# Blocks of tokens turned by 32x32 squares and DMA instead of by TensorE, and two tiles of a macaron transformer block taken in another order

## The chip, the cores and the metric

The kernel runs on one core of one Trainium2 chip. Times are device microseconds (us) of whole executions; the profile and its trace are of one execution, taken by the hardware profiler. TensorE (PE) multiplies matrices, VectorE (DVE) does element-wise work and sums, ScalarE (ACT) activations, GpSimd (POOL) a few small steps, and SyncE (SP) issues most weight transfers. ACT issues transfers too: ACTq in the rows is ACT's sequencer issuing one. A lower time is better.

## The reference

```python
x = x + 0.5 * ffn(layernorm(x), W1, W2, W3)
x = x + attn(layernorm(x), wq, wk, wv, wo, inv_freq)
x = x + 0.5 * ffn(layernorm(x), W1, W2, W3)

def attn(x, ...):                      # x is 4 x 1024 x 512, 16 heads of 32
    q, k, v = x @ wq.T, x @ wk.T, x @ wv.T      # q and k rotated by position
    scores = einsum('bshd,bstd->bsht', q, k) / sqrt(32)   # heads against heads
    return (softmax(scores) @ v) @ wo.T         # of the same token

def ffn(x, W1, W2, W3):                # 512 -> 2048 -> 512
    hidden = silu(x @ W1.T) * (x @ W3.T)
    return fwht(hidden) @ W2.T         # Walsh-Hadamard, folded into W2 beforehand
```

Attention mixes the 16 heads of one token, never two tokens. All is fp32.

## The kernel before

**Work.** The 4096 tokens are 8 tiles of 512; a tile is 4 blocks of 128 tokens. `PASSES` (lines 35 and 36) lists 16 passes; (1, t) is the first feed-forward of tile t and (2, t) its second. I call the p-th entry pass p, from 0. A pass has 16 steps n; in a step PE does `up`, 24 matmuls into PSUM `gu` (gate half, then linear half), and then `down`, 12 matmuls into PSUM `acc`, of the step before. Each fp32 product is three matmuls: every operand is held as a high and a low part, and high-high, high-low and low-high are added.

**A step on the other engines.** When `up` of step n is finished, ACT has made `gated` (silu), DVE multiplies it (line 1584), ACT copies the high part of the hidden tile (line 1084), and DVE makes the low part (line 1591). PE needs the product of step n before `up` of step n + 2, and the low part for the last third of `down` of step n; at the end of a pass, for the whole of the last `down`.

**Attention on DVE.** The attention proper is done by DVE between these, in 512 units (a product and a reduction each, lines 1311 to 1325), three, two or one in a step: `units_by_step` spreads them by a table of costs, in which the other DVE work of a step is weighed too (`beside`, lines 106 to 110). An `exp` on ACT stands between a block's scores and its values.

**Gaps.** Between the passes PE does the projections of the next blocks: `query_key`, `value`, and for one tile `output`. `early_gap` and `late_gap` are the two forms; a pass is `LATE` when it is the second feed-forward of the tile whose attention output is projected in the gap just ahead of it, so that this tile must be normalized and turned inside the gap. Before, LATE is (5, 14, 15).

**Turning.** The projections need features on the partitions, the normalization has tokens there, so each tile and block is transposed once. There are two ways:
- a tile that is not LATE is turned by squares: DVE transposes 32x32 squares (line 1562, steps 8 and 9), ACT issues 16 DMAs from SBUF to SBUF that place them (line 945, four in each of steps 10 to 13), ACT makes the high part (line 952, step 14) and DVE the low one (line 1568, step 15). Attention outputs go the same way, but by a tensor in DRAM, `out_squares`: DVE transposes in place, ACT writes (line 957), and four DMAs read runs of 32 numbers (128 B) back (line 966).
- a block of 128 tokens, and everything of a LATE pass, is turned by PE with `transpose_sub` (line 689) and `transpose_bank` (line 669), 4 matmuls with the identity for a block and 16 for a tile; ACT takes the high part from PSUM (line 935), DVE the low one (line 1189). `early_subs(p)` are the first blocks of a gap whose input is there a pass ahead: DVE normalizes them in step 13 (`Q_APPLY`), and PE turns them between the last `up` and the last two `down`.

**The first gap.** POOL makes the low parts of the attention weights (line 1164); the last four of these, for `wo`, stand beside the first `rope` on DVE (lines 1281 to 1294), which rotates q and k.

## Time and profile before

| | |
|---|---|
| median of 3 runs | 2503.42 us (2503.2 to 2503.71) |
| the profiled execution, its own time | 2501.66 us |
| its span in the trace | 2499.8 us |
| PE busy | 2489.7 us (100%), 11111 matmuls |
| DVE busy | 2044.3 us (82%) |
| ACT busy | 530.2 us (21%) |
| DMA, q1 (SP) and q10 (ACT), share of 16 engines | 46.0% and 5.7% |
| TensorE clock granted | full throughout |

In the rows a matmul of 512 columns lasts 0.39 us, but the next one starts 0.227 us after it: they overlap. What a piece of work costs PE is therefore read from starts, not from durations.

### The profile page before, as it was taken

Reading aid. Unit: us, or ns where it says so; the run is one execution under the profiler, and the core shown is the slowest. Engines: PE = TensorE matmul, PEld = TensorE weight load, DVE = VectorE, ACT = ScalarE, POOL = GpSimd, SP = SyncE. Lnnn points to the kernel's source line nnn. Section 1 sums busy time; section 2 is a strip of 40 time slices with the busy share of each in tenths; the row PEclk is TensorE's granted clock in tenths of the full one; section 3 lists DMA queues with packets and bytes.
Section 4 is the critical chain, followed back from the end, with each engine's and each line's share of the span. In section 5 each row is a group of like instructions: output and inputs, shape, how many; then the busy total and the mean of one; then the engine's idle time right before and its main releaser. Section 6 shows DMA issues by size and latency. Waiting matters only on the chain.

```text
span 2499.8 us, 30169 instructions
## 1 busy us (share of the span) xinstructions
PE 2489.7 (100%) x11111; PEld 2061.4 (82%) x11111; DVE 2044.3 (82%) x2602; ACT 530.2 (21%) x796; POOL 63.0 (3%) x109
## 2 busy tenths in 40 slices
PE   9999999999999999999999999999999999999999
PEld 7878888888888888888888888888888888888887
DVE  9569989699786997979969899797986979878711
ACT  3332212222121221222212122122121212211211
POOL 0030000000000000000000000000000000000000
PEclk9999999999999999999999999999999999999999
DMA  9645635455352564645635466454562545535364
GB/s 343 254 188 181 218 145 200 131 202 210 135 201 81 210 216 162 224 131 206 207 109 188 168 229 208 146 220 144 202 221 93 197 148 219 190 107 199 137 219 165
DMA packets 161172, 459.48 MB, mean 184 GB/s; under 512 B 53312, under 2 KB 82240, under 8 KB 127808
## 3 DMA queue, kind: packets, MB, share of 16 engines
q1 hardware_dynamic: 81792, 419.73, 46.0%
q10 hardware_dynamic: 79296, 38.68, 5.7%
q8 instruction: 46, 0.75, 0.1%
q14 instruction: 38, 0.31, 0.0%
HBM read 408.04 MB, written 38.80 MB: 179 GB/s over the span
## 4 chain that ended last, share of the span: by engine, by line
PE 90%; DVE 8%; issue 1%; DMA 0%; ACT 0%; POOL 0%; SPq 0%; DVEq 0%; ACTq 0%; POOLq 0%
PE gu L608 19%; PE gu L610 19%; PE gu L609 19%; PE acc L639 8%; PE acc L640 8%; PE acc L643 8%; PE acc L608 2%; PE acc L610 2%; PE acc L609 2%; DVE scores L1323 1%; DVE mixed L1325 1%; DVE prod L1316 1%; DVE prod L1311 1%; PE acc L736 1%; DVE gated L1584 1%
## 5 line engine op out<-in xcount | busy, mean ns | idle before, releaser
L608 PE MATMUL gu<-xt,w_up 128*128 128x512 f32 x2048 | 798.4, 390 | 0.2
L610 PE MATMUL gu<-xt,w_up 128*128 128x512 f32 x2048 | 796.8, 389 | 0.0
L609 PE MATMUL gu<-xt,w_up 128*128 128x512 f32 x2048 | 796.7, 389 | 0.0
L608 PEld LDWEIGHTS gu<-xt,w_up 128*128 128x128 f32 x2048 | 384.4, 188 | 80.7 <-issue 0.8
L609 PEld LDWEIGHTS gu<-xt,w_up 128*128 128x128 f32 x2048 | 384.4, 188 | 80.0
L610 PEld LDWEIGHTS gu<-xt,w_up 128*128 128x128 f32 x2048 | 384.4, 188 | 79.8
L1584 DVE TENSOR_TENSOR gated<-gated,gu 128x512 f32<-128x512 f32 x240 | 162.8, 679 | 239.8 <-PE gu L610 238.3
L639 PE MATMUL acc<-w_down,hid 128*128 128x512 f32 x896 | 349.6, 390 | 0.0
L640 PE MATMUL acc<-w_down,hid 128*128 128x512 f32 x896 | 348.6, 389 | 0.0
L1084 ACT ACTIVATE hid<-gated 128x512 fp32r<-128x512 f32 x240 | 152.0, 633 | 892.2 <-DVE gated L1584 882.6
L1325 DVE TENSOR_REDUCE mixed<-prod 128x64 f32<-128x1024 f32 x256 | 310.1, 1213 | 0.0
L1311 DVE TENSOR_TENSOR prod<-tok 128x1024 f32<-128x1024 f32 x256 | 309.1, 1219 | 1.0
L1323 DVE TENSOR_REDUCE scores<-prod 128x32 f32<-128x1024 f32 x256 | 309.6, 1213 | 0.0
L1316 DVE TENSOR_TENSOR prod<-scores,tok 128x1024 f32<-128x1024 f32 x256 | 307.6, 1213 | 1.2
L1076 ACT ACTIVATE gated<-gu 128x512 f32<-128x512 f32 x240 | 143.7, 599 | 591.5 <-PE gu L610 588.5
L643 PE MATMUL acc<-w_down,hid 128*128 128x512 f32 x896 | 239.5, 389 | 0.0
L643 PEld LDWEIGHTS acc<-w_down,hid 128*128 128x128 f32 x896 | 168.2, 188 | 35.0
L640 PEld LDWEIGHTS acc<-w_down,hid 128*128 128x128 f32 x896 | 168.2, 188 | 34.6
L639 PEld LDWEIGHTS acc<-w_down,hid 128*128 128x128 f32 x896 | 168.2, 188 | 34.6
L1591 DVE TENSOR_TENSOR hid<-gated,hid 128x512 fp32r<-128x512 f32 x240 | 163.8, 682 | 20.2 <-ACT hid L1084 20.2
L608 PE MATMUL gu<-w_attn,sub_xt 128*128 128x512 f32 x232 | 90.7, 391 | 0.0
L609 PE MATMUL gu<-w_attn,sub_xt 128*128 128x512 f32 x232 | 90.3, 389 | 0.0
(144 smaller groups left out, 1946.8 us busy)
## 6 DMA issues: line engine op xcount, KB each, us to landing
w_up<-up_pairs SPq DMA_DIRECT2D x240, 1024.0 KB, 4.9
w_down<-down_pairs SPq DMA_DIRECT2D x240, 512.0 KB, 3.5
up_pairs<-w_up SPq DMA_DIRECT2D x16, 1024.0 KB, 5.1
xt<-tok ACTq DMA_DIRECT2D x176, 64.0 KB, 4.1
prod<-up_raw SPq DMA_DIRECT2D x16, 512.0 KB, 6.3
down_pairs<-w_attn SPq DMA_DIRECT2D x4, 2048.0 KB, 18.4
out<-x ACTq DMA_DIRECT2D x7, 1024.0 KB, 5.3
x<-x ACTq DMA_DIRECT2D x6, 1024.0 KB, 6.5
```

What stands on the lines that cost most here:

```text
L608: nc.tensor.matmul(o, w_hi, m_hi, start=first, stop=False)
L609: nc.tensor.matmul(o, w_hi, m_lo, start=False, stop=False)
L610: return nc.tensor.matmul(o, w_lo, m_hi, start=False, stop=last)
L639: nc.tensor.matmul(acc[:, s, :], h_hi[:, s * P:(s + 1) * P], hi, start=first, stop=False)
L640: nc.tensor.matmul(acc[:, s, :], h_hi[:, s * P:(s + 1) * P], lo, start=False, stop=False)
L643: ins = nc.tensor.matmul(acc[:, s, :], h_lo[:, s * P:(s + 1) * P], hi, start=False, stop=False)
L1311: return nc.vector.tensor_tensor(prod[:, buf, :].rearrange("p (h t d) -> p h t d", h=2, t=HEADS), wide(q[:, h:h + 2, None, :], 2, HEADS), ...
L1316: return nc.vector.tensor_tensor(prod[:, buf, :].rearrange("p (h d t) -> p h d t", h=2, d=HD), wide(scores[:, g % 2, h:h + 2, None, :], 2, ...
L1323: return nc.vector.tensor_reduce(scores[:, g % 2, h:h + 2, :], prod[:, buf, :].rearrange("p (h t d) -> p h t d", h=2, t=HEADS), AX.X, ALU.add)
L1325: return nc.vector.tensor_reduce(mixed[:, h:h + 2, :], prod[:, buf, :].rearrange("p (h d t) -> p h d t", h=2, d=HD), AX.X, ALU.add)
L1584: nc.vector.tensor_tensor(by_token(gated[:, u, :]), by_token(gated[:, u, :]), from_bank(gu[:, 2 * u + 1, :], p), ALU.mult).then_inc(s_h, 1)
L1591: nc.vector.tensor_tensor(low, gated[:, u, :], high.bitcast(FP32), ALU.subtract).then_inc(s_hid_lo, 1)
```

## The change

Five things are changed.

1. **Early blocks by squares.** DVE normalizes them in step 11 and transposes 32x32 squares in place; ACT writes each block to `sub_squares` in DRAM in step 12, issues four DMAs of 128 B runs for each in steps 13 and 14, and makes the high part in step 15; DVE makes the low part where it did. PE's transposes of these blocks are gone.
2. **Tiles by way of DRAM.** The squares of a tile go to `tile_squares` by one DMA in step 10, and four DMAs of 512 B runs read them back in step 11 in place of 16; the high part is made in step 13.
3. **Order of the passes.** (1, 4) stands ahead of (2, 1), right behind (2, 0), whose place in SBUF tile 4 takes. So (2, 1) no longer follows the projection of its own attention output, and LATE is (14, 15). Passes 5 and 7 are `TWICE`: their input is read from DRAM a second time into `tok[:, 12:16]` in step 2 of the pass before, normalized and transposed in place there, and written to `tile_squares` by four DMAs of 128 B runs instead of one with long runs.
4. **Order in the gaps.** Where the second block of a gap isn't early (passes 2 and 11), its transposes stand behind the whole of `query_key` of the first, and `value` of the first stands ahead of `query_key` of the second. In the late gap the four outputs stand in a row.
5. **POOL** waits for the first `rope` ahead of the low parts of `wo`.

```diff
-PASSES = ((1, 0), (1, 1), (1, 2), (1, 3), (2, 0), (2, 1), (1, 4), (1, 5),
+PASSES = ((1, 0), (1, 1), (1, 2), (1, 3), (2, 0), (1, 4), (2, 1), (1, 5),
           (2, 2), (2, 3), (1, 6), (1, 7), (2, 4), (2, 5), (2, 6), (2, 7))
+TWICE = tuple(p for p in range(1, NP) if PASSES[p][0] == 1 and PASSES[p - 1] == (2, PASSES[p][1] - 4))
+LOAD = 2
-X_STATS, X_APPLY, X_MOVE, X_SPLIT, Q_STATS, Q_APPLY = 6, 8, 10, 14, 10, 13
+X_STATS, X_APPLY, X_KEEP, X_MOVE, X_SPLIT = 6, 8, 10, 11, 13
+Q_STATS, Q_APPLY, Q_KEEP, Q_MOVE, Q_SPLIT = 10, 11, 12, 13, 15
-    beside[Q_APPLY] += 0.55 * len(early_subs(p + 1))
+    beside[Q_APPLY] += 1.25 * len(early_subs(p + 1))
@@ PE, early_gap @@
                 pe.wait_ge(s_h, HT * p)
+                query_key(new[0])
+                pe.wait_ge(s_added, SUBS * p)
                 if is_early(p, 1):
-                    query_key(new[0])
+                    query_key(new[1])
+                    value(new[0])
                 else:
-                    query_key(new[0], lambda: transpose_sub(new[1]))
-                pe.wait_ge(s_added, SUBS * p)
-                query_key(new[1])
-                value(new[0])
+                    transpose_sub(new[1])
+                    value(new[0])
+                    query_key(new[1])
@@ PE, feed_forward, behind the last up @@
-                    pe.wait_ge(s_h, n0 + HT - 1)
-                    for g in early_subs(after):
-                        transpose_sub(g)
                     down_step(last, 0, False, False)
@@ ACT @@
+            def keep_squares(p):
                 act.wait_ge(s_turned, SUBS * MOVED[p] + SUBS)
+                if p in TWICE:
+                    for s in range(SUBS):
+                        act.dma_start(tile_squares.rearrange("p (f s j) -> p f s j", s=SUBS, j=32)[:, :, s, :],
+                                      normed(s).rearrange("p (f j) -> p f j", j=32)).then_inc(s_squares_kept, 16)
+                else:
+                    act.dma_start(tile_squares, turned).then_inc(s_squares_kept, 16)
+            def keep_sub_squares(g):
+                act.wait_ge(s_sub_turned, MOVED_SUBS[g] + 1)
+                act.dma_start(sub_squares[new_subs(next_of(g)).index(g)], sub_normed(g)).then_inc(s_sub_kept, 16)
+            def move_sub(g):
+                later = max(early_subs(next_of(g)))
+                act.wait_ge(s_sub_kept, 16 * MOVED_SUBS[later] + 16)
...
+                for f in range(QUADS):
+                    act.dma_start(sub_split(g)[1][32 * f:32 * f + 32].bitcast(FP32).rearrange("p k (q j) -> p k q j", q=QUADS),
+                                  squares[f]).then_inc(s_sub_moved, 16)
+            def moved_sub_high(g):
+                later = max(early_subs(next_of(g)))
+                act.wait_ge(s_sub_moved, 16 * QUADS * (MOVED_SUBS[later] + 1))
+                high, low = sub_split(g)
+                nc.scalar.activation(high, low.bitcast(FP32), ACT.Copy).then_inc(s_sub_hi, 1)
@@ ACT, step n, behind the high part of the hidden tile @@
-                    if n == HT - 1 and after < NP and after not in LATE:
+                    if after in TWICE and n == LOAD:
+                        act.dma_start(tok[:, 12:16, :], x_v[PASSES[after][1]]).then_inc(s_again, 16)
+                    if after in MOVED and n == X_KEEP:
+                        keep_squares(after)
+                    if after in MOVED and n == X_MOVE:
+                        move(after)
+                    if after < NP and n == Q_KEEP:
                         for g in early_subs(after):
-                            sub_high(g)
+                            keep_sub_squares(g)
+                    if after < NP and Q_MOVE <= n < Q_MOVE + len(early_subs(after)):
+                        move_sub(early_subs(after)[n - Q_MOVE])
                     for g in EXP_BEHIND.get((p, n), ()):
                         exp(g)
-                    if after in MOVED and X_MOVE <= n < X_MOVE + QUADS:
-                        move(after, n - X_MOVE)
                     if after in MOVED and n == X_SPLIT:
                         moved_high(after)
+                    if after < NP and n == Q_SPLIT:
+                        for g in early_subs(after):
+                            moved_sub_high(g)
@@ POOL @@
+                    if m == O and k == 0:
+                        pool.wait_ge(s_rope, 1)
@@ DVE, step Q_APPLY @@
+                            for s, g in enumerate(early):
+                                dve.wait_ge(s_ln, ln_done(key, s))
+                                squares = sub_normed(g).rearrange("p (f j) -> p f j", j=32)
+                                nc.vector.transpose(squares, squares).then_inc(s_sub_turned, 1)
```

**PE, the gap of pass 2.** `gu<-w_attn,sub_xt` is query and key of a block, `acc<-w_attn,sub_xt` its value, `gu<-ident,prod` the transposes of a block. Before, from the end of the first block's query:

```order
885 L609 MATMUL gu<-w_attn,sub_xt 128x512
886 L610 MATMUL gu<-w_attn,sub_xt 128x512
887 L689 MATMUL gu<-ident,prod 128x128 x4
888 L608 MATMUL gu<-w_attn,sub_xt 128x512
889 L609 MATMUL gu<-w_attn,sub_xt 128x512
```

and now, from the end of its key:

```order
896 L630 MATMUL gu<-w_attn,sub_xt 128x512
897 L631 MATMUL gu<-w_attn,sub_xt 128x512
898 L710 MATMUL gu<-ident,prod 128x128 x4
899 L629 MATMUL acc<-w_attn,sub_xt 128x512
900 L630 MATMUL acc<-w_attn,sub_xt 128x512
...
910 L631 MATMUL acc<-w_attn,sub_xt 128x512
911 L629 MATMUL gu<-w_attn,sub_xt 128x512
```

The transposes moved behind query and key of the first block, its value follows them, and the second block's query and key now come last but one.

**ACT, steps 10 to 14 of pass 6.** `gated<-gu` is the silu of a step, `hid<-gated` the high part of the hidden tile, `scores<-scores` the exp. Before:

```order
337 L1084 ACTIVATE hid<-gated 128x512
338 L945 DMA xt<-tok 32x4x128 x4
339 L1076 ACTIVATE gated<-gu 128x512
...
347 L1084 ACTIVATE hid<-gated 128x512
348 L998 ACT_TABLE_LOAD
349 L998 ACTIVATE scores<-scores 128x256
350 L945 DMA xt<-tok 32x4x128 x4
351 L1076 ACT_TABLE_LOAD
352 L1076 ACTIVATE gated<-gu 128x512
353 L1084 ACTIVATE hid<-gated 128x512
354 L952 ACTIVATE xt<-xt 128x1024 x2
```

and now:

```order
352 L958 DMA tile_squares<-tok 2048x1x32 x4
353 L1121 ACTIVATE gated<-gu 128x512
354 L1129 ACTIVATE hid<-gated 128x512
355 L1002 DMA out_squares<-tok 128x512
356 L968 DMA xt<-tile_squares 32x16x128 x4
357 L1121 ACTIVATE gated<-gu 128x512
358 L1129 ACTIVATE hid<-gated 128x512
359 L982 DMA sub_squares<-prod 128x512 x2
...
362 L990 DMA sub_xt<-sub_squares 32x16x32 x4
363 L1043 ACT_TABLE_LOAD
364 L1043 ACTIVATE scores<-scores 128x256
365 L975 ACTIVATE xt<-xt 128x1024 x2
```

The move of the tile became a write and a read one step apart, with a wait between them; the moves of the blocks stand ahead of the exp, and the tile's high part came from step 14 to step 13.

**DVE, step 13 of pass 6.** A unit is a row of `prod<-` and a row of `scores<-prod` or `mixed<-prod`. Before, step 13:

```order
965 L1584 TENSOR_TENSOR gated<-gated,gu 128x512
966 L1323 TENSOR_REDUCE scores<-prod 128x32
967 L1331 TENSOR_REDUCE head_max<-scores 128x16
968 L1332 TENSOR_TENSOR scores<-scores,head_max 128x256
969 L1591 TENSOR_TENSOR hid<-gated,hid 128x512
970 L1339 TENSOR_REDUCE head_sum<-scores 128x16
971 L1340 RECIPROCAL head_sum<-head_sum 128x16
972 L1316 TENSOR_TENSOR prod<-scores,tok 128x1024 x2
973 L1325 TENSOR_REDUCE mixed<-prod 128x64
974 L1225 TENSOR_SCALAR prod<-x,mean_var,rstd 128x512 x2
```

and now:

```order
972 L1661 TENSOR_TENSOR gated<-gated,gu 128x512
973 L1372 TENSOR_TENSOR prod<-tok 128x1024
974 L1384 TENSOR_REDUCE scores<-prod 128x32
975 L1668 TENSOR_TENSOR hid<-gated,hid 128x512
976 L1384 TENSOR_REDUCE scores<-prod 128x32
977 L1392 TENSOR_REDUCE head_max<-scores 128x16
978 L1393 TENSOR_TENSOR scores<-scores,head_max 128x256
979 L1400 TENSOR_REDUCE head_sum<-scores 128x16
980 L1401 RECIPROCAL head_sum<-head_sum 128x16
981 L1377 TENSOR_TENSOR prod<-scores,tok 128x1024 x2
982 L1386 TENSOR_REDUCE mixed<-prod 128x64
```

The two normalizations left step 13 (they stand in step 11 now, with two transposes), a third unit took their place, and `head_sum`, which needs the exp, stands right behind the row that the exp waits for.

## Rows read from the trace of the kernel before

**Rows 1.** Timeline, PE: start, duration, line; two steps of a pass start.

```profile
565.64 0.39 PE L608 MATMUL gu<-xt,w_up 128*128 128x512 f32 x1
573.80 0.39 PE L608 MATMUL gu<-xt,w_up 128*128 128x512 f32 x1
```

**Rows 2.** Timeline, PE: transposes of two blocks and of a tile, what follows.

```profile
1086.58 1.03 PE L689 MATMUL gu<-ident,prod 128*128 128x128 f32 x8
1087.37 0.48 PE L639 MATMUL acc<-w_down,hid 128*128 128x512 f32 x1
1087.68 0.40 PE L640 MATMUL acc<-w_down,hid 128*128 128x512 f32 x1
...
770.54 1.91 PE L669 MATMUL gu<-ident,tok 128*128 128x128 f32 x16
772.21 0.48 PE L608 MATMUL acc<-w_down,hid 128*128 128x512 f32 x1
```

**Rows 3.** Waits of PE over the span: us in total, times, longest.

```profile
PE acc L608 <- DVE hid L1591: 0.8, 2, 0.4
PE gu L689 <- DVE prod L1225: 0.6, 2, 0.4
```

**Rows 4.** Timeline, DVE and PE at the end of pass 6.

```profile
1088.54 0.68 DVE L1584 TENSOR_TENSOR gated<-gated,gu 128x512 f32<-128x512 f32 x1
1089.92 0.69 DVE L1591 TENSOR_TENSOR hid<-gated,hid 128x512 fp32r<-128x512 f32 x1 [0.70 <-ACT hid L1084]
...
1089.28 1.07 PE L643 MATMUL acc<-w_down,hid 128*128 128x512 f32 x4
1090.76 0.47 PE L608 MATMUL acc<-w_down,hid 128*128 128x512 f32 x1 [0.41 <-DVE hid L1591]
```

**Rows 5.** Timeline, PE and DVE at the end of pass 8.

```profile
1412.99 0.39 PE L610 MATMUL gu<-xt,w_up 128*128 128x512 f32 x1
...
1415.10 0.69 DVE L1591 TENSOR_TENSOR hid<-gated,hid 128x512 fp32r<-128x512 f32 x1 [0.70 <-ACT hid L1084]
```

**Rows 6.** Timeline, DVE: a unit and two normalizations; a transpose.

```profile
449.50 1.22 DVE L1311 TENSOR_TENSOR prod<-tok 128x1024 f32<-128x1024 f32 x1
...
451.76 0.99 DVE L1225 TENSOR_SCALAR prod<-x,mean_var,rstd 128x512 f32<-128x512 f32 x2
452.80 0.69 DVE L1584 TENSOR_TENSOR gated<-gated,gu 128x512 f32<-128x512 f32 x1
...
440.19 0.71 DVE L1348 STREAM_TRANSPOSE tok<-tok 128x512 f32<-128x512 f32 x1
```

**Rows 7.** Timeline, PE and DVE: end of a key projection, its rope begins and ends.

```profile
329.90 0.39 PE L610 MATMUL gu<-w_attn,sub_xt 128*128 128x512 f32 x1
...
330.33 0.69 DVE L1281 TENSOR_TENSOR prod<-gu,cos_t 128x512 f32<-128x512 f32 x1 [1.49 <-PE gu L610]
...
333.96 0.42 DVE L1294 TENSOR_TENSOR tok<-prod 128x256 f32<-128x256 f32 x1
```

**Rows 8.** Timeline, POOL, DVE and PE in the first gap.

```profile
165.68 5.38 POOL L1164 TENSOR_TENSOR w_attn<-tok,w_attn 128x512 fp32r<-128x512 f32 x4 [2.08 <-ACT w_attn L1043]
...
168.44 1.50 DVE L1294 TENSOR_TENSOR tok<-prod 128x256 f32<-128x256 f32 x1
...
171.73 0.50 PE L608 MATMUL gu<-w_attn,xt 128*128 128x512 f32 x1 [2.22 <-DVE tok L1294]
```

**Rows 9.** Timeline, ACT: issues of transfers, and the activations that waited for them.

```profile
901.12 2.59 ACTq L945 DMA_DIRECT2D xt<-tok  x4
...
1089.32 0.58 ACTq L966 DMA_DIRECT2D xt<-out_squares  x1
...
1101.52 2.01 ACT L973 ACTIVATE xt<-xt 128x1024 fp32r<-128x1024 f32 x2 [10.66 <-DMA xt<-out_squares]
...
1562.43 0.58 ACTq L966 DMA_DIRECT2D xt<-out_squares  x1
...
1576.82 1.06 ACT L973 ACTIVATE xt<-xt 128x1024 fp32r<-128x1024 f32 x1 [12.84 <-DMA xt<-out_squares]
```

85 lines of the change are left out of this document (54 added, 31 removed).

## The prediction

> **What bounds the kernel now.** PE does: it is busy for 2489.7 of 2499.8 us, and its waits in the whole span are few and small. A matmul of 512 columns starts every 0.227 us: two steps of a pass start 8.16 us apart with 36 matmuls between [rows 1]. So a matmul that is taken off PE is worth what its start to the next start is, as long as nobody makes PE wait instead. I then looked at who comes closest to that. The list of PE's waits names DVE alone: twice 0.4 us for the last low part of a pass, twice for a normalization in a gap [rows 3]. A wait there is counted from the modelled end of a matmul, 0.17 us behind the free slot, so PE lost 0.57 us each time, 1.15 for the first pair and 0.95 for the second. DVE is busy for 82% of the span, and it may lag within a pass: PE needs the low part of step n 2.72 + 5.44 + 1.81 = 10 us behind its `up`, and DVE has it 3.6 us behind the start of the step's product (0.6, a unit of 2.26 [rows 6], 0.7), so some 6 us of lag cost nothing. At the end of a pass there is no such room. The time after is thus: PE's work, less what is removed, plus the moments in which DVE or ACT come too late.
>
> **What leaves PE.** The order of PE's work has 256 transposes before and 128 now: 24 early blocks of 4, and 16 + 16 of pass 5, which is no longer LATE. Eight of them take 0.79 us from first start to the next matmul's, which itself is followed 0.08 us late: 0.87, or 0.109 each [rows 2]. Sixteen take 1.67 + 0.08 = 1.75 us [rows 2]. 96 x 0.109 = 10.5, and 2 x 1.75 = 3.5: **14.0 us** off PE.
>
> **What comes back at the ends of passes.** Before, the transposes of early blocks stood between the last `up` and the last two `down`, and gave DVE time. Let U be the slot behind the last `up`. In pass 6, U is 1086.58; the last low part ends at 1090.61 and PE starts its last `down` 0.15 later, at U + 4.18, where it could have at U + 3.61 [rows 2, 4]. Now it could at U + 2.72 (12 matmuls). In a pass that DVE ends nearly in time, pass 8, U is 1413.22 and the low part ends at 1415.79: PE could start at U + 2.72, with nothing to spare [rows 5]. So every lag of DVE at a pass end that was hidden under 0.87 us of transposes is paid now. How large are the lags? A step's lag is the last one's plus the work of DVE less 8.16 us.
> - Pass 6 keeps its lag: 4.18 - 2.72 = 1.46. There the row that ACT's exp waits for and the one that needs the exp now stand next to each other (third piece of order above), some 0.5 us of exp and semaphores that nothing fills: **1.96**.
> - Passes 5 and 8: step 13 had two normalizations, 1.04 us, and has a third unit now, 2.26 [rows 6]; the steps behind it are full. 1.2 later than pass 8 was before: **1.2 each**.
> - Pass 2, the other stall: its silu waited behind the tile's high part, which now is made a step earlier; DVE's own lag remains: **0.7**. Pass 3 gets its third unit in step 13 as well, with less lag before: **0.6**. Pass 9: 0.15.
> - The other pass ends have lighter last steps, and a margin of 0.0 to 0.2.
>
> Together 5.8 us against 1.15 before: **4.7 us back**. The transposes of the blocks on DVE themselves, 24 of at most 0.71 us [rows 6], 17 us in all, stand in step 11, where the costs now leave one unit in place of three; the lag that they make, some 4 us by the same account, is under the 6 above and gone before the end, except as counted.
>
> **The gaps of passes 2 and 11.** The second block's key now ends only 12 matmuls, 2.72 us, ahead of the first `up`, which needs its rope. A key ends at 330.13 (329.90 and a slot), its rope at 334.38 [rows 7], and PE sees that 0.06 later: 4.31 - 2.72 = 1.6 us of wait, twice, 3.2. The waits for the normalization go, 0.95: **2.25 us back**. In the other gaps `value` of both blocks still stands behind the last key, 5.4 us.
>
> **ACT and its transfers.** For a usual tile, one write with long runs in step 10 has a step to land, and four DMAs replace sixteen: ACT's sequencer took 2.6 us for four before [rows 9], so this costs ACT less, and I cost it at nothing; DVE's lag covers it. The four DMAs of a block stand in steps 13 and 14; the last starts 4.5 us before the end of `up` in the worst pass and is needed, by way of ACT and DVE, 5.4 us behind that end. Nothing again; the price without this cover is the part of a landing that is over 8 us. For passes 5 and 7 (`TWICE`) the write goes in runs of 128 B, 8192 of them. The nearest rows are the reads of `out_squares` in as many runs: 12.2 us from the first issue to the activation that waits for it, 14.4 in the longest of five [rows 9]. In pass 4 ACT gets to the write some 2.0 us (1.3 of lag and the product's 0.7) behind the `up` of step 10; 12.2 of landing and 2.6 of issue later, 16.8, the silu of step 12 starts, ends 0.6 later, and DVE's product is 1.1 us late; light steps behind make that good. With 14.4 it is 3.3 late, of which 2.1 reach the pass end, and in pass 6 another 2.0. From 0 to 4.1 us; I take **0.5**, since the middle value of the rows costs nothing.
>
> **The first gap.** POOL's four low parts run from 165.68 for 5.38 us beside the first rope, whose last rows take 1.50 us instead of 0.42 [rows 7, 8], and PE, free at 169.34, waits until 171.73, 2.4 us (2.22 + 0.17). With POOL behind the rope this wait goes. But POOL then stands beside four normalizations and the second rope. If each of the four waits for a POOL instruction (1.34 us), they end at 174.7, the second rope 3.95 later at 178.65, and PE, busy until 169.34 + 5.44 + 1.75 = 176.6, waits 2.0 again: gain 0.4. If they don't, 2.4. I take **0.4**: the rows show DVE instructions from and to SBUF slowed beside POOL, and normalizations are such.
> The Trainium skill (GPSIMD Engine Reference, the specifications) says that GpSimd shares its SBUF interfaces with VectorE, and contends with its instructions in a 2-port mode or with two SBUF inputs. The slowed rope rows agree, and by it the normalizations, if in that mode, would be slowed too.
>
> **Sum.** 14.0 - 4.7 - 2.25 - 0.5 + 0.4 = 7.0 us. The profiled execution (2501.66, of which 2499.8 span) would become 2494.7; the median of the runs, 1.8 above it, **2496.5**.
>
> **The rivals.**
> 1. *More lag at the pass ends.* ACT's order changed in steps 10 to 14, and every place where its silu or exp comes later than I think adds to a lag that nothing hides now. For 0.5 us more in all 13 ends: six in stall pay 0.5, seven with some 0.2 of margin pay 0.3, 5.1 us: 2501.6. For it: DVE's list of waits for ACT gets longer by construction. Against: ACT is busy 21%. Chance 0.30, for all outcomes within 5 us (0.2%, about what a measurement can tell from no change) of before.
> 2. *Slower.* The place is the silu of step 12 in passes 4 and 6, behind the wait for the 128 B writes. Beyond 14.4 us of landing each us is lost in both passes. The time is that of before when 4.1 + 2 (L - 14.4) reaches 7.5, at L = 16.1, and 0.2% above at L = 18.6; with twice the reads' landing, 24.4, it is 2503.4 - 7.5 + 24.1 = 2520. For it: the trace has no write in short runs. Against: of five groups of reads in such runs none took over 14.4. Chance 0.14.
> The Trainium skill (DMA: Bandwidth & Descriptors, Specifications) has 512 B as the least transfer for line rate, with a read-modify-write below; it speaks against these writes and for this rival. The trace shows reads of 128 B runs alone, 12.2 us for 1 MB, and neither bears the rule out nor refutes it for writes.
> 3. *All of it.* DVE makes up the lags of passes 3, 5, 8 and 9 and the exp of pass 6 is covered: 0.7 + 1.46 - 1.15 = 1.0 back at the ends, 14.0 - 1.0 - 2.25 + 0.4 = 11.1: 2492.3; with the normalizations free of POOL 2490.3. Chance 0.14.
> 4. That the change doesn't do what it says is excluded by the order: the transposes are gone.
>
> **How the numbers follow.** My own case, a gain of 5 to 9.5 us, has 0.42. Faster by over 0.2%: 0.42 + 0.14 = 0.56; within: 0.30; slower: 0.14. The range goes from 2491.0 (between the two ends of rival 3) to 2505.5, which takes in rival 1 and the worst of 0 to 4.1 with it, and leaves rival 2 out.
>
> **What would show it.** In the profile after: 10983 matmuls; PE's waits for the last low part at the ends of passes 2, 3, 5, 6, 8, some 5 us; two waits of about 1.4 us for a rope ahead of the first `up` of passes 2 and 11; a wait of 2 us for the second rope where 2.2 stood for the first. If ACT waits for `tile_squares` for over 8 us in passes 4 and 6, rival 2 is right; if PE waits at all pass ends, rival 1. A slower clock or PE waiting for weights would make all of it wrong.

## The result: 0.6% slower

| | kernel before | changed kernel |
|---|---|---|
| median of the runs, us | 2503.3 | 2517.2 (2515.7 to 2520.1, 4 runs) |
| ratio | | 1.0058, 95% interval 1.0045 to 1.0070 |
| profiled execution, us | 2501.66 (span 2499.8) | 2516.62 (span 2514.8) |
| matmuls | 11111 | 10983 |

The 128 transposes are gone, as forecast, and the span is 15 us longer all the same. The page of the changed kernel shows it on one line: PE is busy for 2487.1 us, only 2.6 less than before.

```profile
span 2514.8 us, 29949 instructions
...
PE 2487.1 (99%) x10983; PEld 2053.3 (82%) x10983; DVE 2062.0 (82%) x2630; ACT 530.5 (21%) x792; POOL 63.7 (3%) x109
```

The list of PE's waits over the span (us in total, times, longest) answers to [rows 3]. Where 0.8 us stood for the last low part of a pass, there are 10.9; 6.5 for a block's low part are new; the third line holds the two ropes that the prediction had, and the one of the first gap.

```profile
PE acc L629 <- DVE hid L1668: 10.9, 5, 3.9
PE gu L629 <- DVE sub_xt L1265: 6.5, 3, 4.0
PE gu L629 <- DVE tok L1355: 4.1, 3, 1.4
```

The end of pass 5 and the gap behind it show the pattern (timeline of SyncE, ACT, DVE and PE: start, duration, engine, line; in brackets the idle time before and what ended it). U, the slot behind the last `up`, is 937.82.

```profile
933.38 5.23 SPq L594 DMA_DIRECT2D w_up<-up_pairs  x2
...
933.86 6.17 ACTq L990 DMA_DIRECT2D sub_xt<-sub_squares  x4
940.13 0.60 ACT L1121 ACTIVATE gated<-gu 128x512 f32<-128x512 f32 x1 [6.02 <-issue]
...
942.15 0.69 DVE L1668 TENSOR_TENSOR hid<-gated,hid 128x512 fp32r<-128x512 f32 x1 [0.69 <-ACT hid L1129]
...
942.99 0.77 PE L629 MATMUL acc<-w_down,hid 128*128 128x512 f32 x1 [2.28 <-DVE hid L1668]
943.55 0.63 PE L630 MATMUL acc<-w_down,hid 128*128 128x512 f32 x1
...
948.19 1.15 ACT L997 ACTIVATE sub_xt<-sub_xt 128x512 fp32r<-128x512 f32 x2 [6.08 <-DMA sub_xt<-sub_squares]
...
949.69 0.77 PE L629 MATMUL gu<-w_attn,sub_xt 128*128 128x512 f32 x1 [2.20 <-DVE sub_xt L1265]
```

Read it in order of time. SyncE asks for 1 MB of `w_up` at 933.38 (its row merges this load and the next one, which begins at 938.3). ACT begins to issue the second block's four moves 0.5 us later, and needs 6.17 us; the first block's four took 2.63 one step earlier, and four moves of the kernel before 2.59 [rows 9]. The silu of step 15 stands behind that issue, 2.2 us late; DVE's last product and PE's last `down` follow, 2.45 us late. The moves land 14.3 us after their first issue; ACT, DVE and then PE, in the gap, wait for them: 2.4 us more. And each wait is followed by matmuls that start 0.43 us apart instead of 0.227. In a table by stretch (busy time of PE, weight loads, DVE, ACT, POOL; granted clock; DMA share; GB/s) the clock is 1.00 before the wait and 0.60 behind it; 1.2 GHz is 0.5:

```profile
930.00:942.00 12.00, 10.71 (x48) 8.53 (x46) 10.39 (x11) 1.75 (x3) 0.00 (x0) 1.00 0.69 218
942.00:946.00 4.00, 3.02 (x7) 2.47 (x8) 0.69 (x1) 0.11 (x1) 0.00 (x0) 0.60 0.90 240
```

In pass 4 the chain starts at the tile's write in runs of 128 B, in pass 6 at the blocks' write, which stands behind the tile's moves in ACT's order:

```profile
727.20 7.33 ACTq L958 DMA_DIRECT2D tile_squares<-tok  x4
...
741.22 2.71 ACTq L968 DMA_DIRECT2D xt<-tile_squares  x4
744.03 0.60 ACT L1121 ACTIVATE gated<-gu 128x512 f32<-128x512 f32 x1 [7.42 <-issue]
...
1072.37 0.83 ACTq L982 DMA_DIRECT2D sub_squares<-prod  x2
...
1082.08 2.64 ACTq L990 DMA_DIRECT2D sub_xt<-sub_squares  x4
1084.75 1.28 ACT L1043 ACT_TABLE_LOAD   x1 [3.65 <-issue]
...
1086.49 0.42 DVE L1400 TENSOR_REDUCE head_sum<-scores 128x16 f32<-128x256 f32 x1 [1.15 <-ACT scores L1043]
...
1099.53 0.50 PE L629 MATMUL acc<-w_down,hid 128*128 128x512 f32 x1 [3.86 <-DVE hid L1668]
```

In pass 4 the tile's move can start 14.0 us after the first issue of the write; ACT waits for it with the silu of step 12 behind. In pass 6 the first block's move starts 9.7 us after the blocks' write, with the exp of step 13 behind, and DVE waits 1.15 us for that exp, on top of the lag that it already has.

PE's starts, set against 0.227 us a slot, give what was lost by place:

| place | forecast | lost | of it behind the wait, at half clock |
|---|---|---|---|
| end of pass 2 / 3 / 9 | 0.7 / 0.6 / 0.15 | 0.7 / 0.2 / 0.25 | |
| end of pass 4 | 0 (and 0.5 for the write) | 4.8 | 1.7 |
| end of pass 5, and gap behind | 1.2, 0 | 4.0, 4.0 | 1.6, 1.7 |
| end of pass 6 | 1.96 | 5.7 | 1.7 |
| end of pass 8, and gap behind | 1.2, 0 | 1.5, 5.9 | 0, 1.7 (the second) |
| ropes in the gaps of 2 and 11 | 3.2 | 3.4 | |
| first gap | gain of 0.4 | gain of 0.95 | |

Ends and gaps lost 27.1 us against 6.3 forecast. With 20.8 more there, 0.2 more for the ropes and 0.55 less in the first gap, the forecast's 7.0 us of gain become 13.5 of loss. Four late starts of 0.3 to 0.5 us in other gaps, 1.7 in all, make up the 15.0 measured.

### The profile page after: what moved, and what is told of

Same layout as the page of the kernel before. It is cut to its first block, busy times and chain, and to the rows that moved or that the text cites. A ratio compares the mean times of both kernels' runs of the same rounds, so it can differ in the third digit from the quotient of the medians.

```text
span 2514.8 us, 29949 instructions
## 1 busy us (share of the span) xinstructions
PE 2487.1 (99%) x10983; PEld 2053.3 (82%) x10983; DVE 2062.0 (82%) x2630; ACT 530.5 (21%) x792; POOL 63.7 (3%) x109
## 3 DMA queue, kind: packets, MB, share of 16 engines
q10 hardware_dynamic: 161280, 69.09, 10.9%
## 4 chain that ended last, share of the span: by engine, by line
PE 78%; DVE 16%; issue 2%; DMA 2%; ACTq 1%; ACT 0%; POOL 0%; DVEq 0%; SPq 0%; POOLq 0%
PE gu L629 17%; PE gu L631 17%; PE gu L630 17%; PE acc L664 6%; PE acc L661 6%; PE acc L660 6%; DVE mixed L1386 3%; PE acc L629 3%; PE acc L630 2%; PE acc L631 2%; DVE scores L1384 2%; DVE prod L1377 2%; DVE prod L1372 2%; DVE gated L1661 1%; DVE hid L1668 1%
```

## The experiments

Theory A at the start: the loss is the block transfers' place: their issue and landing meet the 1 MB load at the end of a pass. Rival B: DVE's lag alone, which grew by two transposes a pass, or the new order of passes. Each time is a median of 4 to 11 runs, and each ratio is against the kernel before on the same chip; the kernel before had medians of 2502.0 to 2503.3 there, so differences of 1.5 us between experiments of different chips say nothing by themselves. A trace is of one execution, and where that one was far from the median I say so.

**One part at a time.** e1_move13 issues the second block's moves in step 13, behind the tile's high part:

```
-if after < NP and Q_MOVE <= n < Q_MOVE + len(early_subs(after)):
-    move_sub(early_subs(after)[n - Q_MOVE])
+if after < NP and n == Q_MOVE:
+    for g in early_subs(after)[:1]:
+        move_sub(g)
...
 if after in MOVED and n == X_SPLIT:
     moved_high(after)
+if after < NP and n == Q_MOVE:
+    for g in early_subs(after)[1:]:
+        move_sub(g)
```

> The kernel after, with the second early block's four transfers issued in step 13, behind the tile's high part, in place of step 14. Theory A (the loss at the ends of passes 5 and 8 is a collision: these transfers, issued 4 us ahead of the end of the last up, meet the two 1 MB w_up loads that SyncE issues 4.5 us ahead of it, so that their issue blocks ScalarE for 5.3 to 6.2 us and they land 14 us later): the waits of the block's high part for its transfers go from 25 us to under 5, PE's waits for the block's low part (6.5 us) go, and the ends of passes 5 and 8 lose some 1.2 us each in place of 8.2 and 7.5. About 13 us less than the kernel after, 2504. Theory B (VectorE's own lag, from the third unit in step 13 and the transposes of the blocks, is what counts): at most 3 us less, 2514 or more.

2515.3, ratio 1.0056 (1.0040 to 1.0073): rival B by the time. But the trace has theory A's signs at its own places: the gap waits behind passes 5 and 8 are gone, these ends lose 1.3 us each, and the ends of passes 2, 4, 6, 7 and 9 lose more than before (2.9, 5.7, 6.3, 1.8, 5.1). So both moves in one step only shifted the loss. The cause was still open.

e2_order takes the old order of passes (no `TWICE`), e3_gap the old order in the gaps, e4_pool adds only GpSimd's wait to the kernel before. Their edits, in this order:

```
-PASSES = ((1, 0), (1, 1), (1, 2), (1, 3), (2, 0), (1, 4), (2, 1), (1, 5),
+PASSES = ((1, 0), (1, 1), (1, 2), (1, 3), (2, 0), (2, 1), (1, 4), (1, 5),
```

```
-    query_key(new[0])
...
-        transpose_sub(new[1])
-        value(new[0])
-        query_key(new[1])
+        query_key(new[0], lambda: transpose_sub(new[1]))
+    pe.wait_ge(s_added, SUBS * p)
+    query_key(new[1])
+    value(new[0])
```

```
+if m == O and k == 0:
+    pool.wait_ge(s_rope, 1)
```

> The kernel after with the old order of the passes: (2, 1) ahead of (1, 4), so that no tile is loaded twice or written in short runs, and pass 5 is late again and transposes a tile and its attention output on TensorE. Theory C (the writes of tile squares in 128 B runs hold ScalarE until step 12 of passes 4 and 6, and that lag is paid at the pass ends with a clock dip behind it): passes 4 and 6 win back 4.8 and 3.7 us, the transposes cost 3.5: about 5 us less than the kernel after, 2512. Theory D (the short runs are harmless, the ends of passes 4 and 6 are late for the reasons of passes 5 and 8): the end of pass 6 stays as late, and the time is that of the kernel after plus up to 3.5, 2517 to 2521.

> The kernel after with the old order in the gaps of passes 2 and 11: the second block's transposes between query and key of the first, and its query and key ahead of the first value. As predicted before (two waits of 1.6 us for a rope against 0.95 us of waits for a normalization): the two waits for the rope go, 2.4 us less than the kernel after, 2514.8. If something else ends the wait of the first up there, nothing changes: 2517.

> The kernel before with one edit: GpSimd waits for the first rope ahead of the low parts of wo. By the trace of the kernel after, where the wait of 2.4 us for the first rope is gone and one of 1.45 us for the normalizations stands ahead of the tile's transposes: 0.9 us less than before, 2502.4. If the normalizations and the second rope paid in full for what the first gains: no change, 2503.3; if GpSimd did not disturb them at all: 2.4 less, 2500.9.

e2_order 2513.2 (1.0046, 1.0028 to 1.0063), e3_gap 2514.7 (1.0046, 1.0030 to 1.0061), e4_pool 2500.95 (0.9994, 0.9984 to 1.0003). None of the three is the loss. e3_gap's 2514.7 is what was expected, but by the ratios it can't be told from the changed kernel. e2_order's runs lie between 2507.8 and 2522.8, and its trace is of one of 2519.9: there the end of pass 4 is free, yet the ends of passes 2, 5 and 6 and the gap behind pass 11 lose 5.2, 8.7, 6.2 and 5.5 us. At the end of pass 5 it is the same collision, and larger: the second block's moves are issued 0.5 us behind SyncE's load and take ACT 10.1 us. The other places of the loss move with the order of the passes. GpSimd's wait gained 1.0 us by the medians, as much as the first gap did in the changed kernel, though the interval just reaches no change.

The runs of e4_pool show a second thing. All eleven lie between 2500.6 and 2501.4, while the kernel before has about half of its runs at 2501.5 to 2502.8 and half at 2503.0 to 2505.2, the upper ones nearly all with a mean granted clock of 0.999 where the lower ones have 1.000. The late start of 2.39 us in the first gap [rows 8] fits as the cause: it is gone in e4_pool, and e8_dip below shows it with a stretch at half clock behind it that costs 1.6 us, the distance of the two groups. So GpSimd's wait is worth some 0.8 us against the lower group and 2.4 against the upper; the 2503.3 of the result is of the upper group, and the profiled execution of before of the lower.

**The collision.** e5_spread moves one load of SyncE (and writes its loop over the passes out for that). At the end of a pass `w_down` 15 had to wait for a free buffer, and the next pass's first `w_up`, whose buffer had been free for some 3.5 us (`up` of step 14 ends at 929.7, the load starts at 933.38), waited behind it:

```
     down_weights(n0, HT - 2, 0)
+    if p < NP - 1:
+        up_weights(n0 + HT, 0, 0)
     down_weights(n0, HT - 1, 1)
```

> The changed kernel, but SyncE asks for the first w_up pair of the next pass one load earlier: ahead of the last w_down load instead of behind it, so it starts when `up` of step 14 ends (some 8 us before U) and not at U-4.5, where the second block's four transfers are issued. No work is left out. Theory A (the issue of those four met that 1 MB load): ACT's issue in passes 5 and 8 falls from 6.2 and 5.3 us to under 3.5, silu of step 15 no longer waits 5 to 6 us for it, the blocks land 8 to 10 us behind the issue instead of 14, the ends of passes 5 and 8 lose at most 1.3 us each and the waits in the gaps behind them go with their half-clock stretches: 11 to 13 us less, 2504 to 2506. Theory B (ACT is crowded in the last steps whatever SyncE loads): issue times stay scattered over 2.6 to 6 us, and the time stays at 2513 or more.

2505.5 (1.0010, 1.0001 to 1.0020): 11.7 us less, where 11 to 13 were expected. SyncE's load is at 928.21 now, the issue takes 2.73, the silu waits for DVE and no longer for the issue, and PE's list has no wait for a block's low part any more:

```profile
928.21 0.33 SPq L594 DMA_DIRECT2D w_up<-up_pairs  x1
...
932.23 2.73 ACTq L987 DMA_DIRECT2D sub_xt<-sub_squares  x4
935.07 0.60 ACT L1118 ACTIVATE gated<-gu 128x512 f32<-128x512 f32 x1 [2.57 <-DVE hid L1665]
```

e10_base_spread, the same edit in the kernel before, is its control.

> The kernel before with SyncE's first w_up pair of the next pass ahead of the last w_down load. No work is left out. Theory A (the pair at U-4.5 hurts only where block transfers meet it, which the kernel before has none of): no change, 2503 +- 1.5. Rival (the late pair is a loss of its own in every version): several us less, and then e5_spread says nothing on the blocks.

2503.1 (1.0001, 0.9991 to 1.0010): nothing. So the late load cost only where block moves met it. Theory A has its first 12 us; how they split between the held issue and the late landing isn't shown, since the edit cures both.

e8_dip prices the half clock alone, in the kernel before:

```
+DELAY = {7: 8, 13: 8, 10: 5, 12: 5}
...
+if n == HT - 1:
+    for i in range(DELAY.get(p, 0)):
+        nc.vector.tensor_reduce(padding[:, 4 * i:4 * i + 4], wide(ident[:, None, :], 1, 4), AX.X, ALU.max)
```

> The kernel before with nothing changed but useless reductions of 512 elements per partition on DVE ahead of the last step's product: 8 of them in pass 7, 5 in pass 13, 3 in pass 10, 2 in pass 12, whose ends had no wait. At 0.65 us each (the 256-element one took 0.42) and 0.5 us of slack, PE waits about 4.9, 2.7, 1.6 and 0.8 us there. Theory A (a wait from some 2.2 us on is followed by a stretch of matmuls 0.43 us apart that costs 1.6 to 1.7 us more): two such stretches, 10.0 + 3.3 = 13.3 us on top of the kernel before. Theory B (the wait costs only itself): 10.0 us, and the matmuls behind it stay 0.22 to 0.23 us apart.

The kernel that ran has 8, 8, 5 and 5 reductions in passes 7, 13, 10 and 12 (26 in its trace, 0.67 us each), not the 8, 5, 3 and 2 of the expectation, so the forecast sums of 10.0 and 13.3 us don't apply; what the matmuls do behind a late start is read from the trace. 2518.9 (1.0063, 1.0046 to 1.0080), 15.8 us more. PE's timeline at the ends of passes 7 and 10, and in the first gap:

```profile
1256.18 0.77 PE L610 MATMUL acc<-w_down,hid 128*128 128x512 f32 x1 [3.72 <-DVE hid L1596]
1256.75 0.63 PE L611 MATMUL acc<-w_down,hid 128*128 128x512 f32 x1
...
1734.86 0.47 PE L610 MATMUL acc<-w_down,hid 128*128 128x512 f32 x1 [2.21 <-DVE hid L1596]
1735.17 0.39 PE L611 MATMUL acc<-w_down,hid 128*128 128x512 f32 x1
...
172.91 0.51 PE L610 MATMUL gu<-w_attn,xt 128*128 128x512 f32 x1 [2.22 <-DVE tok L1296]
173.25 0.49 PE L611 MATMUL gu<-w_attn,xt 128*128 128x512 f32 x1
173.53 0.63 PE L612 MATMUL gu<-w_attn,xt 128*128 128x512 f32 x1
173.96 0.63 PE L610 MATMUL gu<-w_attn,xt 128*128 128x512 f32 x1
```

The start that was 3.9 us late (pass 7) is followed by 13 matmuls at 0.43 us, 2.9 us more; the one 2.4 us late (pass 10) and the one 1.8 us late (pass 12) by none. In pass 13 two waits of 1.99 and 0.34 us, 1.1 us of work between them, were followed by a slow stretch too. 6.8 + 2.4 + 1.8 + 4.2, and 0.5 in the gap behind pass 10, make 15.7, against 15.8 by the medians. In the profiled execution, which was 1.5 above the median, the first gap adds 1.6: its start is 2.39 us late there as it is before [rows 8], and a slow stretch follows, which none did in the profiled execution of the kernel before. So theory A is right in that the slow stretches come without any of the change's transfers, but a late start alone doesn't decide on one. A late step at a pass end can cost nearly twice its wait.

**The short-run write.** e7_long writes tiles 4 and 5 as the others, by one transfer (the numbers of these two tiles then stand in another order; the amount of work is the same); e11_tile keeps all of the change but the blocks, which PE transposes as before.

```
-if p in TWICE:
-    for s in range(SUBS):
-        act.dma_start(tile_squares.rearrange("p (f s j) -> p f s j", s=SUBS, j=32)[:, :, s, :],
-                      normed(s).rearrange("p (f j) -> p f j", j=32)).then_inc(s_squares_kept, 16)
-else:
-    act.dma_start(tile_squares, turned).then_inc(s_squares_kept, 16)
+act.dma_start(tile_squares, turned).then_inc(s_squares_kept, 16)
```

```
-Q_STATS, Q_APPLY, Q_KEEP, Q_MOVE, Q_SPLIT = 10, 11, 12, 13, 15
+Q_STATS, Q_APPLY = 10, 13
...
+    pe.wait_ge(s_h, n0 + HT - 1)
+    for g in early_subs(after):
+        transpose_sub(g)
     down_step(last, 0, False, False)
```

> The changed kernel, but in passes 3 and 5 (which prepare tiles 4 and 5) the tile's squares are written by one transfer with long runs, as in the other passes, instead of four with runs of 128 B. Tiles 4 and 5 then come out in a wrong order; the work is the same in amount. Theory A (the short runs hold ACT for 5.5 to 7.3 us and land 12 to 14 us later): ACT's issue there is under 1 us, the end of the pass that prepares tile 4 loses under 1 us instead of 4.8 with its half-clock stretch, nothing certain at the other: 4 to 6 us less, 2511 to 2513. Theory B (the lag at that end is DVE's own): within 1.5 us of 2517.

> One part of the change alone: the tile's squares through memory in one write and four moves, the new order of passes with tiles 4 and 5 loaded twice, the order within the gaps and GpSimd's wait, as in the changed kernel; the token blocks are transposed on TensorE as before. No work is left out. By the terms of the sum: 3.6 us less for 32 transposes, 1.0 less for GpSimd's wait, 2.25 more for the ropes in the gaps of passes 2 and 11, so 2500.7 if the short-run writes cost nothing and up to 4 us more if the end of pass 4 waits. Theory A (the block transfers make the loss): 2500.5 to 2504.5. Theory B (the new order of passes and its short-run writes make it): 2508 or more.

e7_long 2517.2 (1.0060, 1.0042 to 1.0077): a miss for the whole. At its own place it did what was expected: pass 4 lost nothing. But pass 6 lost 8.9 us instead of 5.7 (the blocks' write landed 12.5 us after its issue, and DVE waited 3.9 for the exp behind it), and the gaps behind passes 5 and 8 lost 5.9 and 6.1, to the collision that e5_spread takes away. e11_tile 2504.2 (1.0005, 0.9995 to 1.0014), 13 us under the changed kernel: the blocks make the loss. It lost 4.6 us in pass 4, 3.5 in step 14 and 1.1 at the end, to the write alone (ACT, and the longer of PE's two waits):

```profile
728.29 8.80 ACTq L966 DMA_DIRECT2D tile_squares<-tok  x4
...
744.95 2.70 ACTq L976 DMA_DIRECT2D xt<-tile_squares  x4
747.68 1.28 ACT L1029 ACT_TABLE_LOAD   x1 [8.50 <-issue]
...
754.79 0.50 PE L661 MATMUL acc<-w_down,hid 128*128 128x512 f32 x1 [2.85 <-ACT hid L1115]
```

**Who issues.** e6_sync gives all writes and moves to SyncE, between its weight loads; e9_mixed only the tile's, so that ACT keeps the blocks'; e12_units is e9_mixed with fewer units in passes 5, 6 and 8. Wherever SyncE moves the tile, its high part is made in step 14.

The first fence is e6_sync (e9_mixed has the lines of the tile alone), the second e12_units:

```
 for j in range(HT - 5, HT):
     up_weights(n0, j, j % 2)
+    if after in MOVED and j == HT - 4:
+        keep_squares(after)
+    if j == HT - 2:
+        for g in early:
+            keep_sub_squares(g)
+        if after in MOVED:
+            move(after)
+    if j == HT - 1:
+        for g in early:
+            move_sub(g)
     down_weights(n0, j - 1, (j - 1) % 2)
```

```
-UNITS_TO = (0, 37, 73, 110, 144, 182, 220, 256, 294, 331, 368, 400, 438, 476, 512)
+UNITS_TO = (0, 37, 73, 110, 144, 181, 218, 256, 293, 330, 368, 400, 438, 476, 512)
```

> The changed kernel, with every write and move of the tile's and the blocks' squares issued by SyncE instead of ACT, between its weight loads: the tile's write behind the load of w_up pair 12, the blocks' writes and the tile's move behind that of pair 14, the blocks' moves behind that of pair 15, and the next pass's first pair ahead of the last w_down load. The tile's high part is made in step 14 instead of 13. No work is left out. Theory A (the loss is ACT held up by issuing: 2.6 to 7.3 us each time, and by contended moments): silu and exp in steps 10 to 15 no longer wait for an issue, the ends of passes 4, 5, 6 and 8 and the gaps behind 5 and 8 lose what DVE's lag alone gives (0.5, 1.2, 2.0, 1.2 us) instead of 4.8, 9.0, 5.7 and 7.4, and 2517.2 falls by 22 to 2495 (2492 to 2500). Theory B (DVE's own lag at the pass ends is the loss, ACT's waits only go with it): the ends keep 2 to 4 us each and the time stays above 2508. A third outcome: SyncE waits for a write, the weight loads behind it come late, and PE waits for s_up_loaded; that would show as waits of PE in L629 with no DVE work before them.

> The changed kernel with SyncE's first w_up pair of the next pass ahead of the last w_down load (as in e5_spread), and the tile's write and move issued by SyncE (behind w_up pairs 12 and 14); the blocks' writes and moves stay on ACT in steps 12 to 14. No work is left out. Theory A (ACT held by issuing is the loss; in e6_sync it was given back because eight block moves took SyncE 10 to 11 us and w_down came late): from e5_spread's 2505.5, 3.9 us less at the end of pass 4, 2.0 around step 12 of pass 11 and its end, some 1.5 at the end of pass 6: 2498 (2495 to 2501), with no wait of PE for w_down. Theory B (writes on SyncE cost what they save on ACT): 2501 or more, with waits of PE for w_down or w_up.

> e9_mixed with one unit of attention less for DVE in pass 5 and one less in pass 6 (37 instead of 38, pass 7 takes 38 instead of 36), one less in pass 8 (37 instead of 38, pass 10 takes 38 instead of 37). No work is left out. Theory A (what is left at the ends of passes 5, 6 and 8 is DVE's backlog, 2.5 us a unit): these three ends lose 1.3, about 4 and 1.3 us less, and 2498 goes to 2491.5 (2489 to 2495). Theory B (the backlog moves on to the ends of passes 7 and 10): these get waits of 1 us or more each and the time stays above 2496.

e6_sync 2501.1 (0.9991, 0.9981 to 1.0001), 16 us less than the changed kernel where 22 were expected: its third outcome is part of it, at least in the profiled execution, which was 5 us above the median. Eight moves behind a load in one queue took SyncE 10.3 us (its timeline, pass 6), and PE's waits have a line for `w_down`:

```profile
1068.57 10.31 SPq L629 DMA_DIRECT2D sub_xt<-sub_squares  x8
```

```profile
PE acc L671 <- DMA w_down<-down_pairs: 5.6, 4, 2.0
```

e9_mixed 2502.8 (1.0000, 0.9990 to 1.0010): pass 4 and 11 are clean, PE waits for no weights, but the ends of passes 6 and 9 lose 4.8 us each. In pass 9 (ACT) the blocks' write was issued 3.6 us after the tile's move, which is now on another queue, and landed 10.7 us later, with the silu and the exp behind it:

```profile
1539.91 0.98 ACTq L984 DMA_DIRECT2D sub_squares<-prod  x2
...
1550.58 2.76 ACTq L992 DMA_DIRECT2D sub_xt<-sub_squares  x4
1553.45 0.60 ACT L1125 ACTIVATE gated<-gu 128x512 f32<-128x512 f32 x1 [7.58 <-issue]
```

e12_units 2510.6 (1.0031, 1.0019 to 1.0042): 7.7 us worse than e9_mixed, not 6.5 better. Pass 5 ended clean and pass 8 within 0.6, but in pass 6 the write landed 11.5 us later and the silu waited 9.3, and passes 6, 7, 9 and 10 lost 7.6, 2.8, 6.0 and 1.0. Passes 7 and 10 are those that took the units over, as theory B has it. A lighter DVE doesn't help against a wait in ACT's queue.

**The blocks ahead of the tile.** e13_first prepares them in steps 4 to 8; e14_first_sync adds e9_mixed's SyncE; e16_first_sync_gap the old order in the gaps; e15_tile_sync is e11_tile with e9_mixed's SyncE and the old order in the gaps.

```
-Q_STATS, Q_APPLY, Q_KEEP, Q_MOVE, Q_SPLIT = 10, 11, 12, 13, 15
+Q_STATS, Q_APPLY, Q_KEEP, Q_MOVE, Q_SPLIT, Q_LOW = 4, 5, 6, 7, 11, 12
...
```

> The changed kernel with the token blocks prepared ahead of the tile instead of behind it: statistics in step 4, normalization and squares in step 5, the write in step 6, the moves in steps 7 and 8, high part on ACT in step 11, low part on DVE in step 12; SyncE and the tile's steps as in the changed kernel. No work is left out. Theory A (the loss is where the block transfers stand: behind the tile's moves, ahead of the exp of step 13 in pass 6, and across the 1 MB load at U-4.5 in passes 5 and 8): no wait of PE in the gaps behind passes 5 and 8, ends of passes 5 and 8 at most 1.3 us each, the end of pass 6 at most 2 instead of 5.7; the end of pass 4 keeps its 4.8. 2517.2 goes to 2501 (2498 to 2504). Theory B (whatever the place, eight more issues on ACT and DVE's extra squares cost it): above 2508.

> e13_first with SyncE's regular order (next pass's first w_up pair ahead of the last w_down load) and the tile's write and move issued by SyncE, as in e9_mixed. No work is left out. Theory A: beyond e13_first the end of pass 4 loses under 0.5 us instead of 4.8: 2496.5 (2494 to 2499), under the kernel before. Theory B: as e9_mixed showed, what is saved on ACT comes back at other ends; 2500 or more.

> e11_tile (blocks transposed on TensorE as before, tile by squares through memory, new order of passes) with the tile's write and move issued by SyncE, SyncE's regular order, and the order within the gaps as in the kernel before. No work is left out. e11_tile lost 2.8 + 1.0 us in pass 4 where its short-run write held ACT for 8.8 us; if that was its only extra cost, this one is at 3.6 (transposes) + 1.0 (GpSimd's wait) under the kernel before: 2498.6 (2497.5 to 2500.5). If SyncE's writes delay the weights, 2501 or more.

> e14_first_sync with the order within the gaps of passes 2 and 11 as in the kernel before. No work is left out. By the rows the ropes' waits of 1.58 + 0.11 us in each of these gaps go and waits of some 0.9 us for the normalization come back: 1 to 1.5 us less than e14_first_sync, 2495.3. If nothing of the two waits shows in the time, the same as e14_first_sync within 0.7.

e13_first 2508.9 (1.0024, 1.0015 to 1.0034): 8 us less, and no wait for a block in a gap, but 2501 was expected. e14_first_sync 2504.6 (1.0007, 0.9998 to 1.0017), not 2496.5. e16_first_sync_gap 2501.7 (0.9996, 0.9986 to 1.0005), 2.9 less, of which the rows show 2.4 (the ropes' 3.4 against 0.95 for the normalizations), as the prediction had it; 1 to 1.5 were expected. e15_tile_sync 2497.2 (0.9978, 0.9969 to 0.9988): 0.3 under the expected range, and faster than before, the first that is. Its span of 2495.4 is 4.4 under the profiled one of before, where 3.5 for the transposes and 1.1 for the first gap make 4.6; the medians differ by more because that of before is of its upper group. e16_first_sync_gap differs from e15_tile_sync by the blocks and is 4.6 us slower. So even ahead of the tile, the blocks still cost more than they save. In e14_first_sync all of it is one line of PE's waits:

```profile
PE acc L649 <- DVE hid L1673: 10.7, 7, 3.6
```

These are the ends of passes 2, 5, 6, 8 and 9 (1.7, 2.1, 5.4, 3.7 and 1.2 with the slow stretches), where DVE comes to step 15 with lag. What is left as the suspect is rival B's: two transposes of squares on DVE in each pass.

**The cause of the rest.** e17_no_turn leaves these transposes out of e9_mixed (the projections then read blocks that aren't turned); e18_chosen carries blocks by squares only in the seven passes whose end has room, on the rest of e15_tile_sync.

```
-        act.wait_ge(s_sub_turned, MOVED_SUBS[g] + 1)
+        act.wait_ge(s_ln, ln_of_sub(g))
...
-                        nc.vector.transpose(squares, squares).then_inc(s_sub_turned, 1)
```

```
-MOVED_SUBS = {g: at for at, g in enumerate(g for p in range(2, NP) for g in early_subs(p))}
+CARRIED = (4, 5, 8, 11, 12, 13, 14)
+MOVED_SUBS = {g: at for at, g in enumerate(g for p in CARRIED for g in early_subs(p))}
```

> e9_mixed with DVE's transposes of the token blocks' squares left out (two instructions of about 0.65 us in each pass that prepares two blocks); the blocks are written and moved as they are, so that the attention's projections get wrong numbers. The units of attention stay in their steps. Theory A (what e9_mixed still loses is DVE's extra work in passes that it never catches up in): the ends of passes 5 and 8 lose under 0.3 us instead of 2.0 and 1.3, those of 2, 6 and 9 about 1.5 less each and the half-clock stretches behind 6 and 9 go: 2502.8 goes to 2495.5 (2494 to 2498). Theory B (ACT's issues and the blocks' transfers are what is left): 2500 or more.

> The blocks carried by squares only in the seven passes whose end has room on DVE in e9_mixed (those prepared in passes 3, 4, 7 and 10 to 13); the others are transposed on TensorE as in e15_tile_sync. Tile, SyncE's order and the order in the gaps as in e15_tile_sync. No work is left out. Theory A (DVE's room at the pass end decides what a block's transposes are worth): e15_tile_sync's 2497.2 less seven times 0.87 us: 2491.1 (2490 to 2493.5), under both kernels. Theory B (the blocks' transfers and issues cost something wherever they stand): 2495 or more.

e17_no_turn 2493.8 (0.9963, 0.9950 to 0.9976): 9.1 us less than e9_mixed for 24 transposes, 15.7 us of DVE's busy time, with all transfers in place. The traces put the gain at the ends of passes 5, 6, 8 and 9 (1.9, 2.6, 0.9 and 3.7 us); 3.0 of it are the two slow stretches of e9_mixed, which are gone. The end of pass 2 keeps its 1.5 us, against the expectation. e18_chosen 2492.1 (0.9956, 0.9943 to 0.9970): 5.1 under e15_tile_sync, by 13 blocks worth 0.437 us each (5.7), and faster than both kernels; its five runs lie within 0.5 us. PE's waits for the last low part, of e17_no_turn and of e18_chosen:

```profile
PE acc L648 <- DVE hid L1664: 4.4, 4, 2.0
```

```profile
PE acc L653 <- DVE hid L1680: 0.9, 2, 0.4
```

## Why the prediction was wrong

2517.2 is outside the range (2491.0 to 2505.5), and on the side that had 0.14. That side isn't a hit for rival 2 either: it wanted both writes to land after more than 16.1 us, and they landed after 14.0 and 12.1.

**Right.** The transposes: 10983 matmuls, and e15_tile_sync and e18_chosen show that 1.75 us a tile and most of the 0.437 a block (5.1 of 5.7) are paid out when nothing takes them back. The ropes: two waits of 1.42 us in the list, 3.4 us lost for 3.2. The ends of passes 2 and 9; pass 3 lost 0.2 for 0.6. GpSimd: e4_pool gained 1.0 for a forecast of 0.4; PE waits 1.2 us for the second rope where the prediction had 2.0, so GpSimd slowed the normalizations less than I took it to. (By [rows 7] the second rope takes 4.05 us, where the working has 3.95; that changes 0.1.)

**The step that failed: "ACT and its transfers".** It costed a block's four moves by their usual issue, 2.59 us, and "nothing again" for both issue and landing. What stood in SyncE's order at U - 4.5 was in the trace of before, here in pass 6, where U is 1086.58:

```profile
1082.13 5.23 SPq L573 DMA_DIRECT2D w_up<-up_pairs  x2
```

The prediction gave the same place for the moves ("4.5 us before the end of `up`"), but the two were not laid side by side. There an issue took 6.2 and 5.3 us, and landing 14 us where 8 was the bound that I had put; e5_spread shows this to be worth 11.7 us. With it gone the changed kernel is at the upper end of the range. I wrote that "the price without this cover is the part of a landing that is over 8 us", and gave it no rival.

**Two more terms of the same step.** The short-run write landed 14.0 and 12.1 us after its issue (16.7 in e11_tile). Rival 2 put the point of "slower" at 16.1 us of landing in both passes; it didn't count that the issue of the writes itself holds ACT, for 7.3 and 5.5 us, with the silu of the next step behind. I took 0.5 of 0 to 4.1; e11_tile measured 4.6 in pass 4 alone, and e7_long showed that the end of pass 6 isn't saved by long runs. The Trainium skill (DMA: Bandwidth & Descriptors, Specifications) speaks against transfers under 512 B. The writes here agree: at the same two places the 1 MB could be read back 14.0 and 12.1 us after its first issue in runs of 128 B, and 7.9 and 5.6 us after it as one transfer in long runs (e7_long). The prediction weighed that rule too lightly. In pass 6 the wait for the blocks' write, ahead of an exp that stood ahead of all moves in the kernel before, was not in the account.

**The multiplier that was missing.** Five starts that came 2.4 to 4.2 us late were each followed by matmuls at half clock that cost 1.6 to 1.7 us, 8.3 in all. No row of the kernel before has such a stretch in a pass, so no sum from its rows could; its runs at a clock of 0.999 were the only hint. e8_dip shows the stretches without any of the change's transfers.

**The lag account was right in kind and short in size.** It had 1.2 us for the ends of passes 5 and 8; e9_mixed, without collisions there, lost 2.0 and 1.3, and e5_spread 1.3 and 1.3. But that the lag of the transposes "is under the 6 above and gone before the end, except as counted" was wrong for passes 6 and 9: there DVE's lag is 3 to 5 us up to step 14, and any late exp comes on top. With the tile's transfers off ACT, e17_no_turn prices DVE's transposes of squares at 9.1 us, nearly as much as the 10.5 that PE is spared for the blocks. What stays open is how these 9.1 split between the lag itself and the writes that leave earlier when DVE is earlier.

## What to carry to other kernels

Moving work from the bounding engine to another pays only where the other has slack at the next point at which it is waited for: choose the places by the lag at that point, as e18_chosen did, and not by the share of busy time. When transfers are added to an engine that also computes, lay their issue times beside every other queue's at the same moment, and look at what stands behind them in that engine's order. A late start of TensorE of 2 us or more can cost more than itself, here some 1.5 us and up to 2.9.

## What the runs showed of the hardware

- Issuing four block moves of 64 KB took ACT 2.6 to 2.8 us in quiet steps, and 5.3 to 6.2 where a 1 MB load of SyncE had begun 0.5 us earlier (the changed kernel, e3_gap, e7_long), once 10.1 (e2_order). Eight of them behind a load in SyncE's own queue took 9.5 to 11.5 us (e6_sync).
- Four writes of 256 KB in 128 B runs held ACT for 5.0 to 8.8 us, and the wait behind them ended 11.8 to 16.7 us after the first issue. Issued by SyncE, the same four held it for 4.3 to 8.0 us and had landed after 8.1 to 11.4. One write of the same 1 MB in long runs held ACT for under 0.5 us and had landed after 5.2 to 9.4.
- A late start of PE is followed by a stretch at 1.2 GHz, or not. Over all traces, behind the first 115 us: of the starts that came 1.3 to 2.0 us late, none was followed. Of 27 that came 2.05 to 3.11 us late, 14 were, and the same place can go either way: the start of 2.39 us in the first gap was followed in e8_dip, and not in the kernel before and in e10_base_spread. Of 23 that came more than 3.3 us late, 22 were; the one that wasn't came 3.65 us late (e3_gap, end of pass 6). The stretch cost 1.3 to 1.9 us mostly, with 8 or so matmuls 0.43 us apart, and 2.3 to 2.9 in seven cases, with 11 to 14.
